# A pre-norm attention and mixture-of-experts layer: new opening sequence, and the feed-forward's preparation issued on a table of steps

## The reference, cut to what matters

```python
x = x + attention(layernorm(x), wq, wk, wv, wo)      # 32 query heads, 8 key/value heads, head size 8
#   scores = q k^T / sqrt(8); keys j with i-128 <= j < i get -1e10; softmax; times v; times wo
x = x + moe(layernorm(x), w_router, wg, wu, wd, sg, su, sd)
#   scores = sigmoid(x w_router^T) for 8 experts; the two best, normalised, weigh
#   silu(x wg^T) * (x wu^T) @ wd^T of these experts (inner size 640)
#   plus two shared experts of the same shape for every row
```

## Time and profile before

| | |
|---|---|
| median of three runs | 999.13 us (998.54 to 999.97) |
| the profiled execution | 1002.57 us, span 1000.8 us, mean granted TensorE clock 0.976 of full |
| PE busy | 896.4 us (90%) |
| ACT busy | 592.5 us (59%) |
| DVE busy | 462.5 us (46%) |
| POOL busy | 322.8 us (32%) |
| first exponential | 73.09 us |
| first product of the shared experts | 547.07 us |
| last product of the shared experts ends | 748.75 us |

### The profile page before, as it was taken

One profiled execution on the slowest core, in us unless ns is written; L12 is line 12 of the kernel. 1 busy time (PEld: TensorE's weight loads), 2 busy tenths in 40 slices (PEclk: granted clock), 3 DMA queues, 4 the chain that ended last, 5 costly groups with the idle time before them and its releaser, 6 DMA issues.

```text
span 1000.8 us, 23830 instructions
## 1 busy us (share of the span) xinstructions
PE 896.4 (90%) x7905; PEld 551.8 (55%) x7906; DVE 462.5 (46%) x808; ACT 592.5 (59%) x792; POOL 322.8 (32%) x422
## 2 busy tenths in 40 slices
PE   3839999999999999999986999999888999999994
PEld 1413333333333333333335898988777788888884
DVE  5734344443444344434344747475872333333332
ACT  2639999999999999999992333333211222222221
POOL 8005344434444444434330000000011454444442
PEclk9979999999999999999997999999999899999998
DMA  4354544455555444422012102501006882655621
GB/s 137 97 170 164 197 145 152 137 184 186 188 186 196 169 152 175 129 80 81 25 54 69 42 23 70 192 0 42 1 6 247 255 249 46 199 139 135 167 37 22
DMA packets 42089, 123.74 MB, mean 124 GB/s; under 512 B 7616, under 2 KB 23104, under 8 KB 35904
## 3 DMA queue, kind: packets, MB, share of 16 engines
q1 hardware_dynamic: 31568, 110.78, 32.0%
q0 software_dynamic: 7008, 9.70, 5.6%
q10 hardware_dynamic: 3472, 2.76, 0.8%
HBM read 74.06 MB, written 49.15 MB: 123 GB/s over the span
## 4 chain that ended last, share of the span: by engine, by line
PE 57%; ACT 19%; DVE 8%; issue 7%; DMA 4%; SPq 2%; POOL 1%; POOLq 1%; DVEq 0%; ACTq 0%
ACT arena L812 16%; PE ps L1591 12%; PE ps L1406 10%; PE ps L1423 10%; PE ps L1519 9%; PE ps L1610 6%; PE ps L1532 4%; PE ps L1601 2%; DMA wr_all<-w_scr 2%; PE ps L1470 1%; ACT arena L808 1%; DVE ps L973 1%; PE ps L1488 1%; SPq L434 1%; POOL arena L669 1%
## 5 line engine op out<-in xcount | busy, mean ns | idle before, releaser
L812 ACT ACTIVATE arena<-ps 128x1024 f32<-128x1024 f32 x384 | 360.8, 1045 | 5.1 <-PE ps L1423 0.4
L669 POOL TENSOR_SCALAR_AFFINE_SELECT arena<-arena 128x512 f32<-128x512 f32 x240 | 194.4, 819 | 309.6 <-PE ps L1423 175.6
L1423 PE MATMUL ps<-arena 128*32 128x256 f32 x4096 | 279.2, 386 | 1.6 <-POOL arena L669 0.5
L1406 PE MATMUL ps<-arena 64*128 64x512 bf16 x1024 | 176.2, 387 | 43.4 <-ACT arena L812 15.5
L1423 PEld LDWEIGHTS ps<-arena 128*32 128x32 f32 x4096 | 104.8, 109 | 120.5 <-issue 67.1
L1591 PE MATMUL ps<-wr_all,x2T 128*128 x648 | 147.6, 369 | 7.3 <-issue 4.3
L1406 PEld LDWEIGHTS ps<-arena 64*128 64x128 bf16 x1024 | 44.8, 93 | 197.8 <-ACT arena L812 128.1
L1591 PEld LDWEIGHTS ps<-wr_all,x2T 128*128 128x128 f32 x648 | 107.4, 192 | 30.3 <-issue 15.6
L1519 PE MATMUL ps<-x2T,wr_all 128*128 (+1 forms) x480 | 118.5, 399 | 2.4 <-DVE arena L1095 2.4
L1519 PEld LDWEIGHTS ps<-x2T,wr_all 128*128 128x128 f32 x480 | 90.1, 193 | 20.7 <-DVE arena L1095 2.8
L703 POOL COPY now_from<-slot_from 128x1 int32 (+1 forms) x36 | 8.3, 230 | 263.0 <-issue 244.3
(11 more groups left out here) (179 smaller groups left out, 795.8 us busy)
## 6 DMA issues: line engine op xcount, KB each, us to landing
w_scr<-wr_all SPq DMA_DIRECT2D x24, 1280.0 KB, 5.0
...
o_scr<-arena SPq DMA_DIRECT2D x128, 32.0 KB, 1.7
...
```

What stands on the lines that cost most here:

```text
L669: nc.gpsimd.affine_select(out=dst, in_=src, compare_op=ALU.is_ge if own else ALU.is_gt, fill=0.0, base=0, pattern=[[0, REP], [-1 if own el ...
L812: nc.scalar.activation(prob[:, SLOT[k], :, :].rearrange("p h q -> p (h q)"), score.rearrange("p b x -> p (b x)"), ACT.Exp, scale=SCALE).th ...
L1406: last = nc.tensor.matmul(ps[:, 2 * BUF[k] + half, :], kst[r0:r0 + HALF, s, kt * P:(kt + 1) * P], qst[r0:r0 + HALF, s, :, a * QW:(a + 1) * ...
L1423: last = nc.tensor.matmul(ps[32 * h:32 * h + 32, 6 + qc, a % 2 * QW:(a % 2 + 1) * QW], vst[:, s, kt, :], prob[:, SLOT[k], h, :], start=(no ...
```

## The change

- **Opening.** The first 512 rows of x come as two DMAs, the first instruction of SP and of ACT. DVE fills `qst` and `kst` ahead of its first normalisation. POOL fills `vaug` after the second normalisation, ahead of `bandmask`, with a semaphore of its own (`vaug_ready`). PE runs 44 transposes of the identity into an unused bank before the first real one, and transposes the next chunk ahead of the values' product.
- **Handover to attention.** The shift's rows become the first of each half of the stacks. On the usual side of the branch DVE and ACT write one row each into both stacks straight from PSUM, and SP raises the stacks' semaphores when they are done. ACT stores chunk 3's parts in SP's place and takes an exponential of one number before. PE waits for `u_bias` only after the first group's opening turns.
- **Feed-forward.** Forty steps are written out, step = 10 c + q. `TURN` gives the step at which the preparation of chunk 1, 2 and 3 begins (-1, 6, 13): inversions from there, projection at +5, transposes at +7, router at +9. The exponential for the routing is at step 23, the routing on DVE at steps 24 to 37, ranks on PE at 27, slot products at 35 and 37. The first up-product starts on ACT's copies alone, with its products reordered so that the low part comes last; the first router is behind it. The first routed tile is transposed ahead of the last two down-products. The first projection waits for the last accumulator only from its third tile. The tile number of a slot comes from an integer shift in place of a comparison with 41 bounds and a sum.

```diff
+STEPS = NSH * KI
+TURN = {1: -1, 2: 6, 3: 13}
+def turned(step, after):
+    return [c for c, x in TURN.items() if step == x + after]
+EXP_STEP, RANK_STEP, TABLE_STEPS = 23, 27, (35, 37)
...
+            b, qc = divmod(c, QC)
+            for m in range(3):
+                eng.wait_ge(a_p2, c * 3 + m + 1)
+                r0, r = (b * (H * HD) + m * P, P) if m < 2 else (b * (KV * HD), KV * HD)
+                rows = (q_rows if m < 2 else k_scr)[:, r0:r0 + r, qc * CT:(qc + 1) * CT]
+                eng.dma_start(rows.rearrange("a r t -> r a t"), parts[0:r, qc, m, :, :]).then_inc(qk_stored[qc], 16)
         @block.sync
         def _(sp):
+            def load_rows(eng, t0, t1, c):
+                eng.dma_start(xres[:, t0:t1, :], x[t0 * P:t1 * P, :].rearrange("(t p) d -> p t d", p=P)) \
+                    .then_inc(x_in[c], 16)
+            load_rows(sp, 0, TPC // 2, 0)
             for one in (*qk_stored, m_scores, shift_stored, *o_stored, c_proj, c_kept, m_shift, s_hid, s_out, e_xT,
                         e_hid, e_hT, e_y, e_xlo, e_mm, *w_stored, a_vsb, a_normax, c_lsb):
                 sp.sem_inc(one, FIRST)
             sp.sem_inc(w_split, 2)
...
+            for c in range(1, NC):
+                load_rows(sp, c * TPC, (c + 1) * TPC, c)
...
-                    x0, r0 = half * (REP // 2 * L), half * HALF
+                    x0, r0 = half * (REP // 2 * L), half * HALF + SHIFT_ROWS
...
-                    r0, n0 = half * HALF + PAIR_ROWS, half * (REP // 2 * KT)
+                    r0, n0 = half * HALF, half * (REP // 2 * KT)
...
             with sp.Else():
+                for s in range(2):
+                    sp.wait_ge(shift_low, s + 1)
+                    sp.wait_ge(shift_high, s + 1)
+                    sp.sem_inc(st_in[s], 32)
                 sp.wait_ge(u_bias, 1)
                 sp.dma_start(shift_scr[:, 0].rearrange("n r q -> n (r q)").rearrange("n (y x) -> n y x", x=512),
                              shift_fill).then_inc(shift_stored, 16)
                 sp.wait_ge(shift_stored, 48 + FIRST)
-                load_shift(0, 0)
-                load_shift(1, 1)
...
-            step(nc.gpsimd.memset(vaug[:, :, :, :], 0.0))
-            nc.gpsimd.memset(vaug[:, :, :, HD:2 * HD], 1.0).then_inc(first_const, 1)
-            nc.gpsimd.memset(qst[:, :, :, :].bitcast(F32), 0.0).then_inc(const, 1)
-            nc.gpsimd.memset(kst[:, :, :], 1.0).then_inc(const, 1)
...
+            pool.wait_ge(a_xn, 2)
+            step(nc.gpsimd.memset(vaug[:, :, :, :], 0.0))
+            nc.gpsimd.memset(vaug[:, :, :, HD:2 * HD], 1.0).then_inc(vaug_ready, 1)
...
+            act.dma_start(xres[:, TPC // 2:TPC, :], x[TPC // 2 * P:TPC * P, :].rearrange("(t p) d -> p t d", p=P)) \
+                .then_inc(x_in[0], 16)
...
+            store_parts(act, NC - 1)
             act.wait_ge(u_top, 1)
             nc.scalar.activation(norm_row[0:1, 3:4], norm_row[0:1, 2:3], ACT.Sqrt).then_inc(u_root, 1)
+            act.wait_ge(const, N_CONST)
+            nc.scalar.activation(exp_of_one[0:1, :], ones_row[0:1, 0:1], ACT.Exp)
+            act.wait_ge(u_shift, 1)
+            for s in range(2):
+                nc.scalar.copy(qst[HALF:HALF + 1, s, :, :].rearrange("p h q -> p (h q)"),
+                               ps[HALF:HALF + 1, 7, 128:129].to_broadcast([1, REP // 2 * L])).then_inc(shift_high, 1)
...
+                    for ahead in turned(step, 5):
+                        root(ahead + (NC + 1))
+                    for ahead in turned(step, 7):
+                        x2_out(ahead)
+                    if step == EXP_STEP:
+                        act.wait_ge(c_lsb, NC + FIRST)
+                        nc.scalar.activation(rt[:, 0, :, :], logits[:, :, :], ACT.Exp, scale=-1.0).then_inc(r_exp, 1)
...
+            for c in range(NC):
+                shared(c)
...
+            nc.vector.memset(qst[:, :, :, :].bitcast(F32), 0.0).then_inc(const, 1)
+            nc.vector.memset(kst[:, :, :], 1.0).then_inc(const, 1)
...
-                dve.wait_ge(x_in[c], 16)
+                dve.wait_ge(x_in[c], 16 if c else 32)
...
+                dve.wait_ge(vaug_ready, 1)
                 dve.wait_ge(a_v, c + 1)
...
+            for s in range(2):
+                nc.vector.tensor_copy(qst[0:1, s, :, :].rearrange("p h q -> p (h q)"),
+                                      ps[0:1, 7, 128:129].to_broadcast([1, REP // 2 * L])).then_inc(shift_low, 1)
+            dve.wait_ge(shift_high, 2)
             nc.vector.tensor_copy(shift_fill, ps[:, 7, 128:129].to_broadcast([P, 512])).then_inc(u_bias, 1)
...
+                nc.vector.tensor_tensor(x2T[:, 1, :, ds(c * CT, CT)], ps[:, 6:8, :],
+                                        x2T[:, 0, :, ds(c * CT, CT)].bitcast(F32), ALU.subtract).then_inc(c_xlo, 1)
                 nc.vector.tensor_copy(xTc, ps[:, 6:8, :]).then_inc(c_xTc, 1)
-                dve.wait_ge(c_xTc, c + 1)
-                nc.vector.tensor_tensor(x2T[:, 1, :, ds(c * CT, CT)], xTc, x2T[:, 0, :, ds(c * CT, CT)].bitcast(F32),
-                                        ALU.subtract).then_inc(c_xlo, 1)
...
+            def ahead_of(step):
+                for i in range(INVERT):
+                    for c in turned(step, i):
+                        invert(c, i)
+                for c in turned(step, 3):
+                    normalize(c)
+                for c in turned(step, 5):
+                    new_rows(c)
+                for c in turned(step, 7):
+                    xT_copy(c)
+                if step == 0:
+                    logits_out(0)
+                for c in turned(step, 9):
+                    logits_out(c)
...
+                    ahead_of(step)
+                    between(step)
+                if c == NC - 1:
+                    xT_low(0, 0)
...
             merge_pair(NG - 1, 1)
+            invert(0, 0)
+            invert(0, 1)
             merge_pair(NG - 1, 2)
             acc_out(NG - 1, 0)
-            invert(0, 0)
-            invert(0, 1)
...
-            logits_out(0)
-            with dve.Fori(0, NC - 1) as c:
-                shared(c, True)
+            ahead_of(-1)
...
-            xT_low(0, 0)
-                slot, w, tile_no, hot = (slot0, slot1)[k], (w1, w2)[k], wsum, tile_hot[k]
+                slot, tile_no, hot = (slot0, slot1)[k], wsum, tile_hot[k]
-                link(nc.vector.tensor_tensor(from_tile, over_tiles(slot, NTILE + 1),
-                                             tile_starts[:, :].unsqueeze(1).to_broadcast([P, NT, NTILE + 1]), ALU.is_ge))
-                link(nc.vector.reduce_sum(tile_no, from_tile[:, :, 1:], AX))
+                link(nc.vector.tensor_copy(slot_no[:, :], slot))
+                link(nc.vector.tensor_scalar(slot_no[:, :], slot_no[:, :], P.bit_length() - 1, None, ALU.arith_shift_right))
+                link(nc.vector.tensor_copy(tile_no, slot_no[:, :]))
-                link(nc.vector.tensor_tensor(hot[:, :, 1, :], from_tile[:, :, 0:NTILE], from_tile[:, :, 1:], ALU.subtract))
+                link(nc.vector.tensor_tensor(hot[:, :, 1, :], over_tiles(tile_no, NTILE),
+                                             steps[:, :].unsqueeze(1).to_broadcast([P, NT, NTILE]), ALU.is_equal))
...
+            def routing(step):
+                if step == 24:
+                    score_all()
+                if step == 25:
+                    select_first()
+                if step == 26:
+                    select_second()
+                if step == 27:
+                    weigh()
+                    count_rows_first()
+                if step == 28:
+                    count_rows_last()
+                if step == 29:
+                    count_tiles_first()
+                if step == 30:
+                    count_tiles_last()
+                if step == 31:
+                    place()
+                if step == 32:
+                    slot_rows(0)
+                if step == 33:
+                    slot_values(0)
+                if step == 34:
+                    place_rows(0)
+                if step == 35:
+                    slot_rows(1)
+                    slot_values(1)
+                if step == 36:
+                    place_rows(1)
+                if step == 37:
+                    tiles_first()
+                    tiles_last()
+                    slot_table()
...
+            for c in range(NC):
+                shared(c, routing)
             up(0, 0)
...
+            def idle_turns(bank, n):
+                for _ in range(n):
+                    nc.tensor.transpose(ps[:, bank, 0:P], ident[:, :], ident[:, :])
             pe.wait_ge(ident_ready, 1)
+            idle_turns(7, 44)
             transpose_x(0)
...
+                if c + 1 < NC:
+                    transpose_x(c + 1)
...
-            pe.wait_ge(u_bias, 1)
...
+            pe.wait_ge(u_bias, 1)
...
-            pe.wait_ge(acc_free, 2 + NG * QC)
+            pe.wait_ge(acc_free, 2 + NG * QC - 1)
...
+                    if c == 0 and t == TPC // 2:
```

(31 more changed lines are left out.)

138 lines of the change are left out of this document (41 added, 97 removed).

## The result

| | before | after |
|---|---|---|
| median | 999.55 us (998.54 to 999.99, 4 runs) | 980.77 us (980.30 to 982.69, 4 runs) |
| profiled execution, span | 1002.57, 1000.8 | 982.69, 981.0 |
| PE, ACT, DVE, POOL busy | 896.4, 592.5, 462.5, 322.8 | 900.6, 594.4, 462.9, 317.2 |
| mean granted TensorE clock | 0.976 | 0.978 |

The ratio is 0.9817 (95%: 0.9800 to 0.9834): 18.8 us faster by the medians, 19.8 by the two traced spans. I forecast 22.0, 977 us, with a range of 968 to 985. Both traced executions were the longest of their kernel: before's was 3.0 above its median, and the other spans of after are 1.8 to 2.4 us shorter than the traced one.

The account below looks back on a forecast made before the run. Attention was taken as bound by ScalarE and the shared experts by TensorE, with room in the serial opening, feed-forward start and last chunk's routing; 9.4 + 12.6 = 22.0 saved gave a median of 977 us from 999.1, range 968 to 985.

Parts of the forecast that it names:

- Step 1, 2: Opening: earlier x loads start the statistics 3.2 earlier, at 5.3; scalings without GpSimd's fills save 1.0, x normalised by 9.5.
- Step 3: Opening: 44 warm-up transposes raise TensorE's clock and end at 10.1; ScalarE's first read at 14.6 for 20.86, 6.3 saved.
- the turns don't lift the clock: Rival, opening: turns stay at 1.2 GHz, end at 12.3, first read at 19.3, 4.7 less saved, 982; chance 0.17.
- Step 4: Opening: GpSimd's band mask fill collides with VectorE's third normalisation, costing 1.0 (bounds 0 and 3.9).
- Step 5: Opening: the three projection rounds behind the first are unchanged, so the shift is known at 56.1 for 61.40.
- Step 6: Handover to attention: shift copied without going through memory; first merged exponentials from 64.3 for 74.48, 10.2 saved.
- Step 7: Early attention: raw expert weights come late, their split delays a merge that ScalarE wants; 0.8 lost (0 to 2).
- Costed at nothing: Side effects taken as free, among them inversions between the last merges, 1.7 each in VectorE gaps of over 3.
- Chain from the indices: Routed start: gathers, expert 1's blocks, last rows' store and fifth gather put the third tile's down-product 34.7 after the indices.
- The stall and the 1.2 GHz at the third tile: Sign at the third routed tile: down-product still stalled and at 1.2 GHz; if the stall is gone, end below 972.
- Routing a step behind: Rival, last chunk: each slot product waits and the indices come 4 to 8 later, 981 to 985; chance 0.13.
- the late fetch in chunks 2 and 3: Rival, feed-forward: sums fetched too late for VectorE's inversions; twice costs 24 and gives 1001; chance 0.03.

Follow-up runs that it names:

- routing_later: Changed kernel with all of the last chunk's routing, from its exponential to the row indices, one step of the shared experts later; 988.32 us.
- no_turns: Changed kernel without its 44 warm-up turns on TensorE; 984.78 us.
- joined3: Changed kernel with more idle turns, inversions and mask later, raw weights and last rows' store earlier, ranks and slot products behind the down-products; 969.26 us.
- invert_after_merge: Changed kernel with the first two inversions of the softmax sums behind the second of the last merges instead of ahead of it; 979.57 us.
- mask_late: Changed kernel with GpSimd's band mask filled only when all four chunks are normalised; 982.33 us.

## Why the prediction was right, and where not

The sum was 9.4 + 12.6 = 22.0. In the traces it was 5.8 up to the end of attention, 11.0 from there to the third tile, 3.0 behind it: 19.8. So the start gave 3.6 less than its 9.4, the feed-forward up to the third tile 1.6 less than its 12.6, and 3.0 came that the sum did not have. That the number lies so near is in part luck: it is a balance of errors that run both ways.

- **Step 1, 2 (statistics at 5.3, normalised 9.5):** 6.2 and 10.1. VectorE's fills of 2048 elements took 1.76 each, near my upper bound, and VectorE stood 0.49 and 0.38 ahead of them, which I left out; so they ended 0.6 past my 5.6. x itself landed 2.9 and 3.5 after its two issues at 0.88 and 0.96, at about 4.5. So the fills set the start of the statistics, and not x, by some 1.7.
- **Step 3 (turns, first read 14.6 for 20.86):** the mechanism was right, and 14.5 to 14.8 is what the traces with 44 turns and the full clock show. The traced one had 16.44. The step that failed is that I let the clock rise at one time and stay up: I took the turns to end at 10.1, with no gap to x. The clock rose sooner, they ended at 8.4, TensorE stood still for 1.77, and the passes took 8.61. My rival "the turns don't lift the clock" is refuted, and with it, for this case, the Trainium skill's rule for transposes (TensorE: Matmul & The Clock Gate, Part 4: PE-mode transpose): 44 of them took 6.70, and not the 10.7 of the lower clock.
- **Step 4 (collision 1.0):** 1.4 to 1.5 where the first passes are at the full clock, and 0.85 in the changed kernel's own trace (1.32 and 0.90 for 0.69 and 0.68), within the bounds of 0 and 3.9. It hit subtractions, the kind of operation that the rule beside it names, and not the normalisation that step 4 had in mind. **Step 5 (the rounds behind unchanged):** wrong; chunk 2's passes, at the full clock before, were partly at 1.2 GHz in all but one trace with 44 turns, 7.0 to 8.6 for 5.56 (in the one, routing_later, it was chunk 1's, 7.26). The turns are not the cause (no_turns 8.50); with idle turns around the sums ahead of them joined3 had 5.56. The new order of transposes and values' product lies between; it was not tried apart. Steps 1 to 5 together: the shift 2.5 earlier in place of 5.3.
- **Step 6 (handover):** from the shift to the merged exponentials 6.6 for the 8.2 that I had. The two fills together took 4.48 as forecast; the branch idled 0.54 and not 1.8.
- **Step 7 (raw weights, 0.8 lost):** 1.7, within its bounds. Start as a whole: 8.0 of 9.4, read where attention runs steadily (498.27 for 506.27 at the same exponentials). The 8.0 is one trace; by the steady exponentials at the start the traces with 44 turns differ by 2.6 (72.00 in invert_after_merge, 74.55 in mask_late).
- **Costed at nothing, the inversions between the last merges:** the step that failed outright. I had counted their 1.7 us each in VectorE's gaps and not asked when their input lands; the first of them waits in order for a DMA, with a merge behind it. 2.2 lost in the trace against before, which had 1.81 of such a wait at another merge; 3.5 won by the edit.
- **First up-product (5.7 earlier apart from the start):** 11.5 - 5.8 = 5.7. **Low clock (2.5):** 5.46 for 2.75, 2.7. **Three routing waits (2.7):** 1.09, 1.68 and 0.81, 3.6. **End of the shared experts (7.3):** 4.7, of which the waits are 0.9 and the clock 0.2; the other 1.5 is left over against my 192.9 us of pure work and was not traced further.
- **Indices (9.9 ahead of the end, 12.7 earlier):** 10.2 ahead, 10.3 earlier, for the same reason. **Chain from the indices (34.7):** 34.0, and one for one by experiment. Third tile 11.0 for 12.7.
- **The stall and the 1.2 GHz at the third tile (said to remain):** gone, 3.0 gained. My list of signs had this one for an end below 972. It came about, and the end was not below 972, for the start's losses covered it. By the trace the chain (34.0) and TensorE's own work end within 0.2 of each other there, so that the stall went is in part chance too: with the indices 3.3 later it is back.
- **Routing a step behind, the late fetch in chunks 2 and 3, no effect:** none came about; no inversion of chunks 1 to 3 waits. A fetch that lands too late was the right mechanism at the wrong place: it struck chunk 0's, at the end of attention.
